# Graph network kernel: the last three source blocks of an edge pass are multiplied bank by bank, with the edge products behind each bank

## The reference, cut to what matters

```python
def _egnn_conv(x, src, dst, edge_attr, W_msg, W_edge, W_root, b):
    msg = x[src] @ W_msg + edge_attr @ W_edge
    agg = jax.ops.segment_max(msg, dst, num_segments=x.shape[0])
    agg = jnp.where(jnp.isneginf(agg), 0.0, agg)
    return agg + x @ W_root + b
c1 = jax.nn.leaky_relu(_egnn_conv(X, src, dst, edge_attr, W1_msg, W1_edge, W1_root, b1))
c2 = jax.nn.leaky_relu(_egnn_conv(c1, src, dst, edge_attr, W2_msg, W2_edge, W2_root, b2))
```

## Time and profile before

| | us |
|---|---|
| median of 3 runs | 2619.41 (2613.77 to 2621.47) |
| the profiled execution's own time | 2614.05 |
| its span, first to last instruction | 2612.3 |
| 13 intervals between passes of convolution 0, span 1627.51 to 2007.80 | 380.29 |
| 13 intervals between passes of convolution 1, span 2136.78 to 2514.83 | 378.05 |

### The profile page before, as it was taken

How to read it: one execution, slowest core, us unless ns; L and a number is a source line. 1 busy time by engine, 2 the same in 40 slices (tenths; PEclk the granted TensorE clock), 3 DMA queues, 4 the chain that set the end, 5 groups by cost and what they waited for, 6 DMA issues and landing times. The chain is left out here.

```text
span 2612.3 us, 54694 instructions
## 1 busy us (share of the span) xinstructions
PE 2108.3 (81%) x21375; PEld 1855.4 (71%) x21375; DVE 1616.7 (62%) x4651; ACT 879.5 (34%) x1209; POOL 1181.3 (45%) x997
## 2 busy tenths in 40 slices
PE   4494579999999999997876977888886578888860
PEld 4232279999999999997872436777776577777760
DVE  7999975555555555574572034766665356676656
ACT  0495510000000000001210005887784067788720
POOL 0200057887878777720000003666564346566641
PEclk9995579999999999998987986999998589999975
DMA  3592012323233223310007822344333034334321
GB/s 127 179 408 107 1 23 20 30 21 30 21 30 26 24 20 30 30 17 7 2 1 313 318 94 69 115 130 130 111 111 111 19 96 131 113 110 128 121 77 28
DMA packets 150904, 227.14 MB, mean 87 GB/s; under 512 B 87649, under 2 KB 109825, under 8 KB 147106
## 3 DMA queue, kind: packets, MB, share of 16 engines
q1 hardware_dynamic: 70994, 186.72, 19.6%
q0 software_dynamic: 74688, 28.51, 11.4%
q10 hardware_dynamic: 5008, 9.07, 1.1%
HBM read 123.37 MB, written 100.84 MB: 86 GB/s over the span
## 5 line engine op out<-in xcount | busy, mean ns | idle before, releaser
L615 PE MATMUL ps<-parts,at 128*128 128x192 f16 x11250 | 948.1, 248 | 23.4 <-POOL at L647 13.4
L615 PEld LDWEIGHTS ps<-parts,at 128*128 128x128 f16 x11250 | 940.3, 99 | 25.6 <-issue 24.0
L1622 PE MATMUL ps<-yparts,source_onehots_c 128*128 128x192 f16 x7000 | 675.5, 253 | 129.8 <-issue 110.0
L1413 POOL DMA_INDIRECT messages_c<-y_table,srci_sb x504 | 495.6, 983 | 571.9 <-DMA y_table<-ytab 259.4
L1622 PEld LDWEIGHTS ps<-yparts,source_onehots_c 128*128 128x128 f16 x7000 | 590.0, 101 | 199.6 <-issue 156.8
L656 POOL DMA_INDIRECT weight_matrix<-w,place x392 | 608.7, 1553 | 162.2 <-issue 95.6
L1441 ACT ACTIVATE source_gaps_c<-sources_spread,unshift 128x1280 f16<-128x1280 f16 x216 | 294.8, 1365 | 19.3 <-PE ps L1622 3.2
L739 DVE SCALAR_TENSOR_TENSOR t<-ps,coef,g 128x96 f32<-128x96 f32 x400 | 127.0, 317 | 250.3 <-PE ps L615 211.6
L1444 ACT ACTIVATE source_onehots_c<-source_gaps_c 128x1280 f16<-128x1280 f16 x216 | 274.4, 1270 | 6.9
L684 ACT ACTIVATE ea_limbs<-ea_in,ea_scale 128x392 f16<-128x392 f32 x32 | 19.9, 621 | 744.0 <-DMA ea_in<-in_eaT 738.8
L1496 DVE TENSOR_SCALAR source_onehots_c<-sources_spread,shift 128x1280 f16<-128x1280 f16 x484 | 264.9, 557 | 0.3
(11 more groups left out here) (359 smaller groups left out, 1540.2 us busy)
## 6 DMA issues: line engine op xcount, KB each, us to landing
weight_matrix<-blank SPq DMA_DIRECT2D x27, 1600.0 KB
weights<-weight_matrix SPq DMA_DIRECT2D x27, 1600.0 KB, 9.6
run_max<-messages_c SPq DMA_DIRECT2D x28, 960.0 KB
ea_c<-edge_limbs SPq DMA_DIRECT2D x28, 896.0 KB
edge_limbs<-ea_limbs SPq DMA_DIRECT2D x128, 98.0 KB
run_max<-messages_c SPq DMA_DIRECT2D x28, 384.0 KB
sources_spread<-sources_by_tile ACTq DMA_DIRECT2D x26, 320.0 KB
messages_c<-y_table,srci_sb POOLq DMA_INDIRECT x504
```

The lines of the kernel that those rows point to most:

```text
L615: mm = nc.tensor.matmul(m.ps[:, bank, 0:2 * D], m.at[:, s, blk * P:(blk + 1) * P], parts[:, s, :], start=(s == 0), stop=(s == NB - 1))
L1413: nc.gpsimd.indirect_dma_start(msg[:, k % 2, j, :], None, d.yt, bass.IndirectOffsetOnAxis(m.srci[:, k * TURN + j:k * TURN + j + 1], 0)).th ...
L1622: mm = nc.tensor.matmul(m.ps[:, i // 2, at:at + 2 * D], hot[:, b, i * P:(i + 1) * P], parts[:, b, :], start=(b == 0 and i % 2 == 0), stop= ...
```

## The change: what it does

The picks of the blocks 0 to 21 stand as they did. The blocks 22, 23 and 24 (`BANKED = 3`) are no longer multiplied block by block over all ten steps and then closed. The new `pick_by_bank` first waits for all three one-hot tiles (and for the edge attributes), then goes bank by bank: the two products of block 22 for this bank, the two of block 23, the two of block 24, and at once the two edge products of this bank, the second of which raises `closed`. Then the next bank. `used` for the three blocks is raised in the last bank. The counts of all instructions stay.

```diff
+            def pick_tile(b, i):
+
+                at = 2 * D * (i % 2)
+                return nc.tensor.matmul(m.ps[:, i // 2, at:at + 2 * D], hot[:, b, i * P:(i + 1) * P], parts[:, b, :],
+                                        start=(b == 0 and i % 2 == 0), stop=False, skip_group_check=True)
...
-            def close(k, odd, half):
-
+            def pick_by_bank(k, odd, half, first):
+
+                for b in range(NB - BANKED, NB):
+                    onehot_made(k, first, b)
+                if first:
+                    pe.wait_ge(wscaled, 1)
                 pe.wait_ge(eal[odd], 16 * half + 16)
-                for i in range(PICKS):
-                    at = 2 * D * (i % 2)
-                    mm = nc.tensor.matmul(m.ps[:, i // 2, at:at + D], ea[:, odd, i, :], wl[:], start=False,
-                                          stop=(i % 2 == 1), skip_group_check=True)
-                    if i % 2:
-                        mm.then_inc(closed, 1)
+                for bank in range(PBANKS):
+                    for b in range(NB - BANKED, NB):
+                        for i in (2 * bank, 2 * bank + 1):
+                            mm = pick_tile(b, i)
+                        if bank == PBANKS - 1:
+                            mm.then_inc(used, 1)
+                    for i in (2 * bank, 2 * bank + 1):
+                        at = 2 * D * (i % 2)
+                        mm = nc.tensor.matmul(m.ps[:, bank, at:at + D], ea[:, odd, i, :], wl[:], start=False,
+                                              stop=(i % 2 == 1), skip_group_check=True)
+                    mm.then_inc(closed, 1)
...
-                        for b in range(done, upto):
-                            pick(k + 1, 1 - odd, half + odd, False, b)
+                        for b in range(done, min(upto, NB - BANKED)):
+                            pick(k + 1, False, b)
                         done = upto
                 if more:
-                    close(k + 1, 1 - odd, half + odd)
+                    pick_by_bank(k + 1, 1 - odd, half + odd, False)
```

More of the change, by code:

```diff
@@ L80 @@
 SPLIT_B = 13
+BANKED = 3
 EPS = 1e-5
@@ L1606, in _, with onehot_made @@
         def _(pe):
-            def pick(k, odd, half, first, b):
+            def onehot_made(k, first, b):
                 if first and b in ACT_FIRST:
@@ L1617, in pick @@
                     pe.wait_ge(hotv, made_by_vector(k, b))
+            def pick_tile(b, i):
+                at = 2 * D * (i % 2)
+                return nc.tensor.matmul(m.ps[:, i // 2, at:at + 2 * D], hot[:, b, i * P:(i + 1) * P], parts[:, b, :],
+                                        start=(b == 0 and i % 2 == 0), stop=False, skip_group_check=True)
+            def pick(k, first, b):
+                onehot_made(k, first, b)
                 for i in range(PICKS):
@@ L1620, in pick @@
                         pe.wait_ge(picked, PBANKS * k + (i // 2 + 1 - PBANKS))
-                    at = 2 * D * (i % 2)
-                    mm = nc.tensor.matmul(m.ps[:, i // 2, at:at + 2 * D], hot[:, b, i * P:(i + 1) * P], parts[:, b, :],
-                                          start=(b == 0 and i % 2 == 0), stop=False, skip_group_check=True)
+                    mm = pick_tile(b, i)
                 mm.then_inc(used, 1)
-            def close(k, odd, half):
-                pe.wait_ge(eal[odd], 16 * half + 16)
-                for i in range(PICKS):
-                    at = 2 * D * (i % 2)
-                    mm = nc.tensor.matmul(m.ps[:, i // 2, at:at + D], ea[:, odd, i, :], wl[:], start=False,
-                                          stop=(i % 2 == 1), skip_group_check=True)
-                    if i % 2:
-                        mm.then_inc(closed, 1)
+            def pick_by_bank(k, odd, half, first):
+                for b in range(NB - BANKED, NB):
+                    onehot_made(k, first, b)
+                if first:
+                    pe.wait_ge(wscaled, 1)
+                pe.wait_ge(eal[odd], 16 * half + 16)
+                for bank in range(PBANKS):
+                    for b in range(NB - BANKED, NB):
+                        for i in (2 * bank, 2 * bank + 1):
+                            mm = pick_tile(b, i)
+                        if bank == PBANKS - 1:
[5 more added lines that the diff above has]
+                    mm.then_inc(closed, 1)
             def edge_terms(k, odd, half, first, e):
@@ L1655, in turn @@
                         upto = -(-(e + 1) * NB // NEG)
-                        for b in range(done, upto):
-                            pick(k + 1, 1 - odd, half + odd, False, b)
+                        for b in range(done, min(upto, NB - BANKED)):
+                            pick(k + 1, False, b)
                         done = upto
                 if more:
-                    close(k + 1, 1 - odd, half + odd)
[L1662 to L1665, removed]
+                    pick_by_bank(k + 1, 1 - odd, half + odd, False)
+            for b in range(NB - BANKED):
+                pick(0, True, b)
+            pick_by_bank(0, 0, 0, True)
             turn(0, 0, 0, True, True)
```

## The result

| | before | after |
|---|---|---|
| median (lowest to highest), 4 runs each | 2620.44 us (2613.77 to 2622.96) | 2578.4 us (2576.4 to 2580.81) |
| span of the profiled execution | 2612.3 us | 2576.1 us |
| 13 pass intervals, convolution 0 | 380.29 us | 362.31 us |
| 13 pass intervals, convolution 1 | 378.05 us | 362.93 us |

The ratio is 0.9844, 95% interval 0.9831 to 0.9857: 42 us faster, and 18 us better than the forecast of 2596. The time lies outside the forecast's own range of 2585 to 2609 and inside the wide one of 2567 to 2624. The span fell by 36.2 us, and the 26 intervals carry 17.98 + 15.12 = 33.1 of them, 1.27 us each. Up to the first convolution and behind the last one the two traces agree within 1 us. The stretch from the last copies of convolution 0 to the first ones of convolution 1 fell from 128.98 (2136.78 - 2007.80) to 126.16 us.

The account below looks back on a forecast made before the run. TensorE was taken as nearly full in the convolutions, busy 24.8 of 29.2 us a pass, the rest pauses. Restarts 18, clock 3 and ends 2 make 23 us off 2619.4: 2596, own range 2585 to 2609, wide range 2567 to 2624.

Parts of the forecast that it names:

- (a): Restart of a pass: banks close apart, so copies run earlier; gain 1.15 us, between 0.55 and 1.53.
- the 2.15 us: Lag from the last edge product's recorded end to ScalarE's first copy; draining work by the skill's rule, which no reordering removes.
- (b): TensorE's pauses inside the pass take back part of the restart gain; 0.6 kept, 0.69 us a restart, 18 us in all.
- (c): TensorE's clock, at 0.50 behind the restart pause: shorter pauses spare a fifth of 13 us, 3 us.
- (d) to (g): Ends of the two convolutions 2 us; waits for one-hot tiles, POOL's later last gather and PSUM's alternating products 0 each.
- Slower through bunched gathers: Rival: three POOL gathers bunched at each restart hold TensorE up; 2628 us, or 2653 at full cost; chance 0.15.
- Nothing kept: Rival: restart gets shorter and TensorE's inner pauses longer by as much; 0 to 6 us, 2613 to 2620; chance 0.26.
- All kept: Rival: the whole restart gain stays, 40 us, with clock 13 and ends 4; 57 us, 2562; chance 0.21.
- A against B: Experiments' theories: gain from spread closings with copies beside TensorE (A), or from last blocks' order or POOL's held gather (B).

Follow-up runs that it names:

- Set 3: Picks of blocks 13 to 18 doubled in the kernel before, the changed kernel, and the changed one with only block 24 by bank: 2521.26, 2487.62, 2501.24 us.
- set 4: Changed kernel with picks of blocks 13 to 18 doubled and all ten edge products behind the fifth bank: 2631.77 us, ratio 1.0061.
- set 1: Changed kernel with closings at the end (twice), or one or five blocks by bank; kernel before with 20 more products a pass: ratios 0.9994 to 1.0002.

## Why the prediction was right

**(a) The copies: right in kind, too small in size.** The copies were at the low end of the step's span, one ahead and four bunched, for which I had reckoned a gain of 0.55 us; I took 1.15 and held 1.53 for the most. The restart pauses shrank by 1.94, more than that most, though the steps of 0.38 us were to shrink to one or two and most restarts still have four. What I left out is that the lag itself could move. The first copy of a pass began 2.28 us after its bank's close before and 1.32 us after it now (means of 26). The last copy began 3.67 us after its bank's close before and 1.58 now; of these 1.5 and 1.1 us are the copies queued ahead of it on ScalarE. The sum had counted only the copies' pitch. The Trainium skill, page Perfetto Trace Analysis (section Tensor Engine Instruction), says that a product's recorded end is computed from its size and that its semaphore goes out after PSUM has acknowledged. By that rule, as I read it, the 2.15 us were work still draining and would have stayed. They did not stay at the restart. Some turned up ahead of the first close, where the last ten products before it now have 1.4 us of pauses a pass and had 0.1. (ScalarE's one-hot work had ended 2.6 us before the last close, not 2.4; nothing hangs on it.)

**(b) What comes back: right, and the larger effect.** Of 1.94 us won at the restarts 1.56 came back as pauses inside the pass. TensorE had 1.94 + 0.85 = 2.79 us a pass more at hand, with the clock, and kept 1.23, which is 0.44 where I took 0.6. Set 3 shows the other end: where nothing lags, 1.12 us are kept whole. So the return belongs to whatever holds TensorE up on the first chip and not to the change.

**(c) The clock: the term that was mis-sized.** I counted 3 us, with 13 as the upper end. All of the clock lost, 26.5 us by rows 2, came back (1.00 in both windows), 0.85 us a pass at the products' pitch, 22 us in all. How the 33 us of the intervals divide isn't shown, as the clock and the pauses changed together. If the clock's part is kept whole, it is 22 us and the copies' is 10; if both are kept at 0.44, it is 10 and 22. The forecast of 23 us is 13 short of the 36.2 in the span. The clock's term is 7 to 19 us short on either division, while the 18 us for the copies may be too many or too few. That the sum of two terms off in size came so near is in part luck.

The Trainium skill, page TensorE: Matmul & The Clock Gate (section Why this matters for your kernels), has it that idle gaps between bursts bring the clock down. The sum by that rule was 10 us better, which is nearer the result, and the trace agrees: pauses of 2 us with steps behind them stood before the stretches at 1.2 GHz, and where the restart pauses add up to 1.3 us in small pieces these stretches are gone. More time is lost in pauses inside a pass than before, in smaller pieces, and the clock stays at 2.4 GHz.

**(d) to (g).** The forecast had 2 us for the ends of the two convolutions and none for the first passes. The stretch between the two convolutions gave 2.8 us, half of it behind the last copies of convolution 0 and half in the first pass of convolution 1. Behind the last copies of convolution 1 there was nothing (97.44 and 97.45 us). So the total fits better than its parts. Nothing was seen to wait for the one-hot tiles, and products alternating between closings and picks keep the pitch (0.66 us for six picks at 2252.18 above). POOL's gathers did bunch as forecast, in its timeline after:

```profile
2250.58 0.95 POOL L1414 DMA_INDIRECT messages_c<-y_table,srci_sb  x1 [1.17 <-remote]
2251.83 0.95 POOL L1414 DMA_INDIRECT messages_c<-y_table,srci_sb  x1 [0.30 <-issue]
2253.89 0.95 POOL L1414 DMA_INDIRECT messages_c<-y_table,srci_sb  x1 [1.12 <-PE ps L1622]
2255.14 0.94 POOL L1414 DMA_INDIRECT messages_c<-y_table,srci_sb  x1 [0.30 <-issue]
2256.39 0.95 POOL L1414 DMA_INDIRECT messages_c<-y_table,srci_sb  x1 [0.30 <-issue]
```

**The rivals.** "Slower through bunched gathers" fell: with those gathers about, TensorE's first 3 us of the next pass are full (36 products in 2.93 us at clock 1.00). "Nothing kept" was right in its mechanism for four fifths of the restart's gain and wrong as a whole. "All kept" was wrong on the first chip, at 36 of its 57 us, and right in set 3.

**What stays open.** What makes TensorE's signals lag by some 2 us in the kernel before where it takes 2614 us, and by 0.1 us on the faster chips and, with 60 more products a pass, on the chip of set 4; and whether the pauses spared or the clock carries more of the gain. I had no order-before and closings-at-end pair without added products on a chip that lags, so A against B is shown by time in set 3 alone, and by the place of the steps in set 4. The kernel before itself was not traced on the faster kind of chip, only its variants.

## What to carry to other kernels

Find the late engine before pricing a wait at a hand-over: the same wait is worth 1.12 us where the multiplying engine sets the time and nothing where the gathers do. The engine that sets the pace of one hand-over (ScalarE in set 1) needn't be the one that sets the time. Look for the engine that has no gap from the first to the last instruction of the stage, and at what ends last. When one engine fills several banks that another has to clear, close them one by one, at a spacing above the clearing engine's pitch (0.58 us against 0.38 did it, 0.25 did 60% of it). Where products pause inside a block for no named reason, count most of a spared wait as coming back, but look at what stood at half clock behind it, for that can come back in full.

## What the runs showed of the hardware

I had not expected that the same kernel takes about 2407 us on two chips and 2616 to 2620 us elsewhere. The difference lies in the convolutions: the interval is 23.9 us where it was 29.2, and copies start within 0.1 us of a close once ScalarE is free. It shows beside the gathers. In the first pass of convolution 1, with gathers back to back, TensorE recorded 27 products in 12.76 us. That is from 7.1 us behind the first gather on; up to then its products show no pause. At the same distance behind the first gather, on a chip of the faster kind (the changed kernel, POOL at nearly the same pitch):

```profile
2005.92:2018.68 12.76, 12.76 (x168) 12.76 (x166) 9.08 (x26) 12.31 (x14) 9.71 (x11) 1.00 0.19 42
```

Here it is 168 products, 20 or so of them the shorter edge products, in the same 12.76 us without a pause. It isn't only the picks. Behind convolution 0, where POOL again gathers at 1.25 us, 50 products (L1692) that VectorE reads out of PSUM are spread over 31.1 us in the kernel before and over 8.3 us on the faster kind. VectorE waits for them up to 9.78 us at a time, where 1.5 is the longest there:

```profile
2058.07 1.41 DVE L1568 TENSOR_SCALAR stream_selector<-ps,col 128x512 f32<-128x512 f32 x2 [9.78 <-remote]
```

So on the one kind of chip TensorE's work or its signals are late beside gathers at this pitch, and on the other not; why, no run here shows.
